# Gate and up of a decoder layer's feed-forward net as Strassen block products, seven for eight

## What is computed

```
def _L0_ffn_ref(x, w_gate, w_up, w_down):        # x: 2048 x 512, w_gate, w_up: 512 x 2048
    h = silu(x @ w_gate) * (x @ w_up)
    h_sparse = _sparsify_2to4(h)     # of each 4 neighbours keep the 2 of largest magnitude
    return h_sparse @ w_down
x = _layernorm(x + _L0_ffn_ref(x, w_gate, w_up, w_down))
```

## Time and profile before

| | |
|---|---|
| three runs | 1091.35, 1091.44, 1092.93 us; median 1091.44 |
| profiled execution, first to last instruction (span) | 1090.9 us |
| TensorE busy | 1037.0 us, 95% |
| VectorE, ScalarE, GpSimd busy | 738.5, 486.3, 294.7 us |
| mean granted TensorE clock | 0.992 of full speed |
| DMA moved | 106.18 MB |

### The profile page before, as it was taken

How to read it: one execution, slowest core, us unless ns; L and a number is a source line. 1 busy time by engine, 2 the same in 40 slices (tenths; PEclk the granted TensorE clock), 3 DMA queues, 4 the chain that set the end, 5 groups by cost and what they waited for, 6 DMA issues and landing times.

```text
span 1090.9 us, 18063 instructions
## 1 busy us (share of the span) xinstructions
PE 1037.0 (95%) x6022; PEld 839.6 (77%) x6023; DVE 738.5 (68%) x1769; ACT 486.3 (45%) x905; POOL 294.7 (27%) x496
## 2 busy tenths in 40 slices
PE   7889998999999885999999999999999999999996
PEld 6667776777777664888888888888888888888885
DVE  5898699778868986566747546545565536654666
ACT  5688488758857884222324222131222122221124
POOL 2186348545733641223210006000000000000224
PEclk9999999999999998999999999999999999999998
DMA  8877267727743732224541003210020000100102
GB/s 260 237 200 204 78 199 200 197 83 188 199 117 117 207 143 77 79 77 164 175 162 61 1 1 40 39 39 1 1 77 12 27 0 33 45 1 1 39 27 89
DMA packets 55216, 106.18 MB, mean 97 GB/s; under 512 B 6240, under 2 KB 8288, under 8 KB 55136
## 3 DMA queue, kind: packets, MB, share of 16 engines
q1 hardware_dynamic: 50256, 90.99, 29.7%
q0 software_dynamic: 4880, 14.18, 3.4%
HBM read 72.11 MB, written 30.94 MB: 94 GB/s over the span
## 4 chain that ended last, share of the span: by engine, by line
PE 57%; DVE 2%; ACT 1%; issue 0%; DMA 0%; POOL 0%; POOLq 0%; DVEq 0%
PE f_bank L53 55%; PE f_bank L1714 1%; PE f_bank L1722 1%; PE f_bank L1793 1%; PE f_bank L1738 0%; DVE ln_stats L1104 0%; DVE rows_kept L2150 0%; ACT rows_kept L1132 0%; DVE h L2116 0%; DMA rows<-sorted_dram 0%; DVE rows_kept L2139 0%; DVE h L2056 0%; DVE rows_kept L1111 0%; POOL out L1660 0%; ACT fsg L1936 0%
## 5 line engine op out<-in xcount | busy, mean ns | idle before, releaser
L1896 ACT ACTIVATE fsg<-f_bank 128x512 f32<-128x512 f32 x64 | 38.2, 598 | 295.6 <-PE f_bank L53 289.2
L2056 DVE TENSOR_TENSOR h<-f_bank,fsg 128x512 f32<-128x512 f32 x64 | 44.2, 691 | 181.6 <-PE f_bank L53 181.4
L714 ACT ACTIVATE probs<-bank,nmax 128x384 f32<-128x384 f32 (+3 forms) x256 | 131.7, 549 | 21.4 <-DVE nmax L899 19.3
L883 DVE CUSTOM_DVE_ANT_0 bank<-bank,mask 128x384 f32<-128x384 f32 (+3 forms) x256 | 122.9, 502 | 13.8 <-PE bank L510 13.0
L521 PE MATMUL bank<-ident,probs 128*128 128x128 f32 x640 | 108.7, 284 | 24.6 <-DVE pt_lo L908 10.7
L1137 POOL TENSOR_SCALAR ln_var<-ln_mv 128x1 f32<-128x1 f32 x39 | 8.9, 229 | 438.8 <-DVE ln_mv L1106 437.4
L908 DVE TENSOR_TENSOR pt_lo<-bank,pt_hi 128x512 f16<-128x512 f32 (+1 forms) x192 | 114.7, 598 | 16.7 <-ACT pt_hi L724 16.4
L724 ACT ACTIVATE pt_hi<-bank 128x512 f16<-128x512 f32 (+1 forms) x192 | 104.9, 546 | 23.5 <-PE bank L521 22.9
L53 PE MATMUL bank<-x_hi,w_qk 128*128 128x512 f32 x256 | 101.5, 414 | 6.7 <-DVE x_lo L913 6.3
L53 PE MATMUL f_bank<-wd_hi,hs_lo 128*128 128x512 f32 x256 | 100.0, 391 | 0.0
L53 PE MATMUL f_bank<-wd_lo,hs_hi 128*128 128x512 f32 x256 | 99.9, 390 | 0.0
(11 more groups left out here) (275 smaller groups left out, 2445.7 us busy)
## 6 DMA issues: line engine op xcount, KB each, us to landing
big_lo<-q_hi_dram SPq DMA_DIRECT2D x32, 256.0 KB
big_lo<-q_lo_dram SPq DMA_DIRECT2D x32, 256.0 KB
big_lo<-k_hi_dram SPq DMA_DIRECT2D x32, 256.0 KB, 3.8
big_lo<-k_lo_dram SPq DMA_DIRECT2D x32, 256.0 KB, 5.1
rows<-sorted_dram SPq DMA_DIRECT2D x19, 256.0 KB, 2.6
q_hi_dram<-q_hi SPq DMA_DIRECT2D x16, 256.0 KB, 3.0
q_lo_dram<-q_lo SPq DMA_DIRECT2D x16, 256.0 KB, 2.9
k_hi_dram<-k_hi SPq DMA_DIRECT2D x16, 256.0 KB, 3.5
```

Source lines behind the costliest of these rows:

```text
L714: ins = act.activation(probs[u % RP][:, at:at + cols(r)], S[u % SR][:, at:at + cols(r)], ACT.Exp, bias=nmax[:, r, c:c + 1])
L883: dve.tensor_tensor_reduce(out=S[u % SR][:, at:at + cols(r)], in0=S[u % SR][:, at:at + cols(r)], in1=mask[:, T - cols(r):T], scale=1.0, sc ...
L1896: act.activation(fsg[v % 2][:, :], GB[v % 2][:, :], ACT.Silu).then_inc(s_sg, 1)
L2056: dve.tensor_tensor(h[r % 2][:, j, :], UB[v % 2][:, :], fsg[v % 2][:, :], ALU.mult).then_inc(s_h, 1)
```

## The change

**Seven products for eight.** Two token blocks are taken together, r = 2p and 2p + 1, and the contraction of 512 is cut in two of 256. Gate and up of one group of 128 columns over both blocks is then a 2 x 2 by 2 x 2 product of blocks, each elementary product contracting over 256 (6 matmuls). Instead of eight there are seven, m1 to m7, of sums and differences of blocks. On the weight side these are the two gate halves (G01, G23), four sums S1 to S4 and one up half (U23), seven pieces of 256 columns in all; on the token side the pieces B11, B21, B22 and the sums T1 to T4. A unit u is one group j of one chunk for one pair p: 2 x 4 x 4 = 32 units, in eight sets k of four (p = 0 for k < 4, p = 1 from MID = 16 on).

The seven go into three kinds of banks. In bank AB m1, m6, m7 and m4 are accumulated one on another, and ScalarE copies the bank out after the first three (copy1 to g0, copy2 to g1, copy3 to v1); m2 goes to BB; m5 and then m3 to CB. VectorE adds: c11 = m2 + g0 (gate of the first block), c22 = m5 + v1 (up of the second), c12 = m5 and m3 + g1 (gate of the second); up of the first block is AB after m4. ScalarE applies silu0 and silu1; product0 on VectorE and product1 on GpSimd make h of the two blocks.

```
+            def group(g):                      # TensorE
+                m1(g)
...
+                m2(g)
...
+                if g >= 1 and g != MID + 1:
+                    m4(g - 1)
+                for y_tile in outers(g, 0):
+                    outer(*y_tile)
+                if g == MID - 1:
+                    turn_piece(1, B21)
+                if g >= 1 and g != MID + 1:
+                    m3(g - 1)
+                m6(g)
...
+                    m5(g)
...
+                for y_tile in outers(g, 1):
+                    outer(*y_tile)
...
+                m7(g)
```

```
+        def outers(g, place):
+            k, j = g // J, g % J
+            if j == 0 and place == 0 and k >= 2:
+                return [(k - 2, 6), (k - 2, 7)]
+            if j == 2 and place == 1 and k >= 1:
+                return [(k - 1, 0), (k - 1, 1)]
+            if j == 3 and k == NK - 1:
+                return [(k - 1, 2)] if place == 0 else []
+            if j == 3 and k >= 1:
+                return [(k - 1, 2 + 2 * place), (k - 1, 3 + 2 * place)]
+            return []
```

**ScalarE**, in one group, in this order (the cuts of MID and of unit 0 left out):

```
+                    copy3(g - 1)
+                    up_hi(g)
+                    fourth_hi(g)
+                    if g + 1 < U:
+                        gate_hi(g + 1)
+                    copy1(g)
+                    if g + 1 < U:
+                        sums_hi(g + 1)
+                    if j == 1 and k >= 1:
+                        magnitudes(k - 1)
+                    if j == 3 and k >= 1:
+                        kept_hi(k - 1, 1, 0)
+                    silu0(g)
+                if j == 0 and k >= 1:
+                    fourth_magnitude(k - 1, 0)
+                copy2(g)
+                if j == 1 and k >= 1:
+                    for half in range(2):
+                        kept_hi(k - 1, 0, half)
+                if j == 3 and 1 <= k < NK - 1:
+                    kept_hi(k - 1, 1, 1)
+                silu1(g - 1)
+                if j == 1 and k >= 1:
+                    down_hi(k - 1)
+                if j == 3:
+                    first_magnitudes(k, 0)
+                if g in (25, 29):
+                    first = g - 25
+                    for t in range(first, first + RW):
+                        normed_early(t)
```

```
+                up_lo(g)
+                fourth_lo(g)
+                if g == U - 1:
+                    last_down_lo()
+                if g + 1 < U:
+                    weight_sums(g + 1)
+                    gate_lo(g + 1)
...
+                if g + 1 < U:
+                    sums_lo(g + 1)
...
+                if g >= 1:
+                    product1(g - 1)
...
+            for g in range(U):
+                group(g)
+                if g in (24, 28):
+                    first = g - 24
+                    for t in range(first, first + RW):
+                        ln3.rstd(pool, t, t % 8)
+                if g == 25:
+                    pool.wait_ge(s_order_in, 16)
+                if g >= 26:
+                    write(g - 26)
```

**The end.** Behind group 31 stand on TensorE: tile (6, 3), m4 and m3 of unit 31, tiles (6, 4) to (6, 7), and the eight tiles of set 7. VectorE chooses set 7 in four half blocks of 256 tokens:

```
+            c22(U - 1)
+            product0(U - 1)
+            add_up(last - 1, 3)
+            kept_lo(last - 1, 1, 1)
+            c12(U - 1)
+            compare_fourth(last, 0, 0)
+            count_wins(last, 0, 0)
+            choose(last, 0, 0)
+            add_up(last - 1, 4)
+            kept_lo(last, 0, 0)
...
+            choose(last, 1, 1)
+            add_with_sum(0)
+            kept_lo(last, 1, 1)
+            add_with_sum(2)
```

More of the change, by code:

```diff
@@ L1463, in late @@
     NS = N // P + E - 1
-    RING = weights.RING
     RR = 4
@@ L1620, in step @@
                     if n == EARLY:
-                        for i in range(RING):
-                            weights.load(sp, i, i, (gate, up)[i % 2][0, i // 2])
+                        weights_in(0)
+                        weights_in(1)
                         block_in(0)
```

1070 lines of the change are left out of this document (720 added, 350 removed).

## The result

The kernel after takes 1207.32 us (1205.52 to 1208.27), against 1091.97 before (four runs each): ratio 1.1057, 95% interval 1.1041 to 1.1072. The forecast was 1145.0, in a range from 1082 to 1168: slower, as said, but by 115 us instead of 53. The profiled execution has a span of 1203.8 us, 59.5 over the 1144.3 of the sum.

A forecast was written before the change was run, and what follows sets the result against it. TensorE's count of matmuls was taken as the bound. Against the profiled execution: 1090.9 - 43.7 + 5.2 + 34.8 + 7 + 19 + 19.5 + 2 + 5.8 + 3.8 = 1144.3 us, given as 1145; range 1082 to 1168.

The forecast's parts named there:

- The two unit waits: In steady sets TensorE waits for copy2 at j = 1 (2.5 us) and copy3 at j = 2 (3.2): +34.8 over k = 2 to 7.
- The start's waits: Before unit 0's products on T2 and T3, TensorE waits 6.6 and 10.7 us for GpSimd's rows; whole start +19.5.
- Units 25 and 29: First-half layer norm: four rstd delay GpSimd's sums, four normalisations delay copy3 in these units; together +19 us.
- rival 2: Narrow GpSimd operations cost half, 0.35 us for 256 columns, giving 1112 us; chance 0.13.
- Loading the weights twice and straight code: 24 MB of weights loaded for 12, and loops unrolled; both taken to cost nothing.
- the sixteen order scatters: Token-number scatters moved into the expert loop, in GpSimd's idle 3.4 us at a time; taken at nothing.
- Rival 3: VectorE and GpSimd hinder each other: 1153 us if choose is held back by product1, 1166 with sums and start stretched; chance 0.15.
- the middle, +5.8: Units 15 to 17, turning the second half's pieces: waits of 1.5 (B11), 3.9 (B22) and 0.4 us (unit 17).
- the clock, +2: The gap at the start cools TensorE's clock, about 2 us lost.
- the tail, +3.8: After unit 31, VectorE's compare, count and choose chains make the third kept half 1.8 us late, fourth 1.4, last additions 0.6.

The follow-up runs named there:

- the best order: Kernel after with ScalarE's queue reordered, scatters in three bunches, layer norm spread, start and middle reordered, unit 15's subtractions and the tail's high half moved: 1151.49 us.

## Why the prediction was wrong

**Right.** The sign and its reason: TensorE loses 43.7 us of matmuls and waits for the three engines behind it. The two unit waits were placed where they are and put at 2.5 and 3.2; in unit 9 and at the head of unit 10 they are 1.42 and 2.86. A set forecast at 65.8 measured 67.7: its waits come to 5.4 us (5.8 forecast), and the rest, some 2 us, is slow clock, which filling the waits did not shorten. The start's waits (6.6, 10.7) measured 6.0 and 10.4. Units 25 and 29 took 8.4 and 10.1 us over the 16.5 of their like, with 8.9 and 10.1 forecast, and spreading the norm gave back 13.5 us in those units, of the 19. 256-wide GpSimd operations take 0.70 from start to start when alone (0.69 forecast), so rival 2 falls. Loading the weights twice and straight code, taken at nothing, show no wait of TensorE behind the loop. Idle time forecast: 34.8 + 7 + 19 + 19.5 + 5.8 + 3.8 = 89.9; measured 101.6 - 9.3 = 92.3, and 2.5 us more of T2's wait that lie ahead of 569.60. That it agrees so closely is partly luck, as the next points show.

**Wrong, one: "the sixteen order scatters move between the expert scatters, where GpSimd sits idle 3.4 us at a time".** The step priced GpSimd's issue time and not the DMA. Its price is 16.6 us in the trace of the kernel after (12.6 to 23.4 in the seven other kernels with this loop) and 23.8 by itself in the kernel before, by delay of other queues' loads; three bunches elsewhere give 14.6 back. The working asked which engine is idle, when the rows of the loop hinge on a load that must land in 2.6 us.

**Two: VectorE and GpSimd.** Rival 3 had the mechanism and was left out of the sum; at 1153 to 1166 its price was near what a steady set took over the forecast (1.23; measured 1.9, whose cause no run isolates), but it named one place where it bites. It bites at many: units 1 to 7, the two 1024-wide subtractions beside choose (7.37 for 2.50), and the win counts of unit 16 (two rows of 2.59 and 2.71 us, which take 0.42 and 0.69 alone, each beside one 1024-wide subtraction of GpSimd). Moving one pair of operations was worth 4.0 us in unit 15 (6.3 in the best order).

**Three: "the middle, +5.8".** Units 12 to 19, with the middle among them, came to 17.9 more. Of that the waits are 6.5 for the second half of B11 (1.5 forecast), 7.0 for B22 (3.9) and 4.1 ahead of unit 17's products (0.4). The hindrance of point two is the cause of about half of the first (6.5 became 3.2 when the subtractions were moved). For the wait for B22 the trace shows those two long counts (860 to 865 us) ahead of c12, and behind c12 ScalarE's silu1, then the high and the low half of T3: the chain that the forecast had, with counts 4.2 us longer. No run took them away, and the wait in unit 17 was not followed up.

**Four: "the clock, +2".** The slow clock is 41.0 us of busy time instead of 2.1, and the idle time agreed with the forecast only because the working counted it at full clock. As a term of its own it is worth about 5, by the places that the run with filled waits shortened, and not the 39 that the difference of clocks suggests; the rest lies mostly under the pace of the other engines.

**Five: "the tail, +3.8".** The chain of compare, count and choose was as forecast, the fourth half's wait was put at 1.4 and was 4.64, because ScalarE's queue at that place was not read: two squares and two normalisations stand ahead of the high half. The experiment gives back 3.0 us of the tail's 9.8 over the forecast. For the other 6.8 the trace has waits of 0.85 and 0.76 where none was forecast and one of 3.08 for 1.8, and some 4 us of slow clock from 1174 us on; no run took these away.

Shown by a run and by its trace are the loop (16.6 of the 59.5 us, 15.2 of it given back), the hindrance in unit 15 (4.0), the clock (about 5) and ScalarE's queue in the tail (3.0), some 29 us in all. The other 30 lie in units 1 to 7, the middle, the sets and the tail, where the long rows of VectorE and GpSimd are. The run with less work for GpSimd, 18.8 us shorter behind the loop, speaks for the hindrance there, but it took work away too; that the hindrance is all of the 30 was argued from rows, not shown.

## What to carry to other kernels

Fewer matmuls pay only while the chain of the other engines is shorter than TensorE's time per unit; so write out that chain before the saving, with every operation that stands ahead in each queue. When work is moved to an idle engine, ask what it shares with others: GpSimd operations that read SBUF cost the VectorE operation beside them up to their whole length (choices of 2.50 us took 4.13, 6.91 and 7.37), and a scatter of small elements delayed loads of other queues that were under way. Before a difference of a few us is put down to an edit, read in the trace whether it arose at the edit's place: here the median fell by 6.1 us and the tail by 3.0. A slow granted clock behind a wait is a price only where TensorE sets the pace; fill the wait to see.

## What the runs showed of the hardware that I had not expected

- Indirect scatters of 128 four-byte elements landed after 9.0 us (median) with loads beside them, and 256 KB loads of another queue then took 8.9 to 21.4 us where they had taken 2.6 to 2.8.
- Three VectorE comparisons with two SBUF operands stood for 66.65 us while GpSimd issued additions back to back, and took 3.50 beside memsets. In unit 27 four unedited choices took 4.50 us beside GpSimd operations of 1.17, and in another execution 6.91 beside the same operations at 0.75.
- After a wait of only 2.86 us (to 730.94) the granted clock was 0.50 from 732 to 734 us and 0.70 from there to 736; it stayed at 1.00 after waits of 1.14 and 1.42 us (717.94 and 723.68).
